# Softmax over window offsets on all 128 partitions of stage 3, with spreads on four row tiles and without GpSimd

## The reference

```python
qkv = x @ w_qkv
starts = jnp.arange(0, L - KS + 1, ST)          # KS = 4, ST = 2
idx = starts[:, None] + jnp.arange(KS)[None, :]
win = qkv[:, idx]
...
dots = jnp.einsum('bnqhd,bnkhd->bnhqk', q, k) * scale
attn = jax.nn.softmax(dots, axis=-1)
o = jnp.einsum('bnhqk,bnkhd->bnqhd', attn, v)
y = o @ w_out + b_out
out = out.at[:, idx.reshape(-1), :].add(y.reshape(B, N * KS, C))
```

## Time and profile before

| | |
|---|---|
| median of 3 executions | 803.98 us (803.6 to 805.56) |
| the profiled execution | 795.91 us, span 794.1 us |
| PE busy | 718.8 us (91%) |
| DVE busy | 492.0 us (62%) |
| ACT busy | 398.2 us (50%) |
| POOL busy | 109.0 us (14%) |
| mean granted TensorE clock | 0.975 |

### The profile page before, as it was taken

How to read it: one execution, slowest core, us unless ns; L and a number is a source line. 1 busy time by engine, 2 the same in 40 slices (tenths; PEclk the granted TensorE clock), 3 DMA queues, 4 the chain that set the end, 5 groups by cost and what they waited for, 6 DMA issues and landing times.

```text
span 794.1 us, 18851 instructions
## 1 busy us (share of the span) xinstructions
PE 718.8 (91%) x7725; PEld 372.5 (47%) x7725; DVE 492.0 (62%) x1136; ACT 398.2 (50%) x732; POOL 109.0 (14%) x103
## 2 busy tenths in 40 slices
PE   6899999986999878999968869999998899999996
PEld 3454545453555543444426445555655334443332
DVE  0673544445889867667557876666664666728552
ACT  2737474735676753434442324656554435553454
POOL 1380313120000000000023544112110000000000
PEclk9999999998999999999977999999999999999998
DMA  8400000000000013552200000000000000000000
GB/s 352 168 4 1 3 0 3 1 4 1 2 2 0 1 30 80 108 109 61 47 0 1 1 0 1 2 4 4 3 4 3 0 1 0 0 1 0 14 14 26
DMA packets 6863, 21.00 MB, mean 26 GB/s; under 512 B 576, under 2 KB 576, under 8 KB 6272
## 3 DMA queue, kind: packets, MB, share of 16 engines
q1 hardware_dynamic: 6784, 19.88, 8.7%
HBM read 18.70 MB, written 1.18 MB: 25 GB/s over the span
## 4 chain that ended last, share of the span: by engine, by line
PE 66%; DVE 16%; ACT 7%; issue 7%; DMA 2%; POOL 1%; DVEq 0%; SPq 0%; ACTq 0%
PE bank L1771 5%; PE bank L2370 4%; PE bank L2296 4%; PE bank L2009 4%; PE bank L1802 3%; PE bank L2349 3%; PE bank L2306 3%; PE bank L1997 3%; PE bank L2002 3%; PE bank L2131 2%; PE bank L1815 2%; DVE sb_rowmax L1135 2%; PE bank L2192 2%; PE bank L2196 2%; PE bank L2285 2%
## 5 line engine op out<-in xcount | busy, mean ns | idle before, releaser
L1771 PE MATMUL bank<-sb_xT,sb_arena 128*128 128x512 f32 x128 | 58.9, 608 | 6.5 <-DMA sb_arena<-w 6.5
L887 ACT ACTIVATE sb_arena<-bank 128x512 f32<-128x512 f32 x64 | 34.8, 607 | 48.5 <-PE bank L2162 48.5
L1451 DVE TENSOR_REDUCE sb_rowmax<-bank 128x4 f32<-128x512 f32 x64 | 41.2, 685 | 23.6 <-PE bank L2153 23.6
L616 ACT ACTIVATE sb_arena<-bank 128x512 f32<-128x512 f32 x64 | 36.1, 601 | 28.3 <-PE bank L1771 28.1
L1065 DVE TENSOR_TENSOR sb_arena<-bank,sb_arena 128x512 f32<-128x512 f32 x32 | 20.9, 686 | 46.0 <-PE bank L1815 46.0
L791 ACT ACTIVATE sb_arena<-bank 128x512 f32<-128x512 f32 x36 | 21.5, 597 | 47.4 <-PE bank L1997 47.4
L531 POOL TENSOR_TENSOR sb_arena<-sb_la,sb_consts 128x1024 f32<-128x1024 f32 x16 | 31.6, 1982 | 88.7 <-PE bank L1802 69.3
L1771 PEld LDWEIGHTS bank<-sb_xT,sb_arena 128*128 128x128 f32 x128 | 24.7, 195 | 37.4 <-issue 35.7
L1684 DVE TENSOR_TENSOR sb_arena<-sb_arena,bank 128x512 f32<-128x512 f32 x32 | 21.0, 683 | 29.7 <-PE bank L2353 22.0
L2009 PE MATMUL bank<-sb_arena,sb_w 128*128 128x512 f32 x72 | 36.0, 600 | 3.0 <-DVE sb_arena L1352 3.0
L742 ACT ACTIVATE sb_arena<-sb_arena 128x512 f32<-128x512 f32 x32 | 20.1, 629 | 35.6 <-DVE sb_arena L1140 35.5
(11 more groups left out here) (338 smaller groups left out, 1602.5 us busy)
## 6 DMA issues: line engine op xcount, KB each, us to landing
sb_arena<-weights_by_expert SPq DMA_DIRECT2D x16, 512.0 KB, 8.0
sb_w<-w SPq DMA_DIRECT2D x1, 2646.5 KB, 22.4
sb_w<-w SPq DMA_DIRECT2D x1, 1736.0 KB, 16.3
sb_consts<-consts SPq DMA_DIRECT2D x1, 1404.0 KB, 10.6
sb_arena<-w SPq DMA_DIRECT2D x2, 512.0 KB, 5.5
sb_ctxT<-ctx SPq DMA_DIRECT2D x1, 1024.0 KB, 12.5
out<-sb_xT SPq DMA_DIRECT2D x4, 256.0 KB, 2.5
sb_xT<-x SPq DMA_DIRECT2D x1, 768.0 KB, 7.9
```

What stands on the lines that cost most here:

```text
L616: act.activation(BC[:, n, :], bank[(4, 5, 0, 1)[n % 4]][:], ACT.Copy).then_inc(s_vev, 1)
L887: act.activation(probT4[k % 2][:, g].rearrange("p b j q -> p (b j q)"), by_key[g][:], ACT.Exp).then_inc(s_e4, 1)
L1451: dve.tensor_reduce(rowmax4[k % 2][:, 4 * g:4 * g + 4], bank[n][:].rearrange("p (j t) -> p j t", j=4), AX, ALU.max).then_inc(s_mx4, 1)
L1771: pe.matmul(bank[(4, 5, 0, 1)[n % 4]][:], bc_w_tiles[:, n, :], cols(c), start=True, stop=True).then_inc(s_v, 1)
```

## The change

In stage 3 only, but for the loop:

- A chunk is cut into 16 blocks of 32 tokens. The head sums put block 4j + s (j column tile, s = 0 to 3) on partitions 32j + 8s to 32j + 8s + 7, so that all 128 partitions hold useful numbers, and an offset takes 32 columns of one bank. The sums of one offset are 16 matmuls of 32 columns, four of which (s) add into the same 32 partitions, each with a stationary matrix that is zero but for its 8 of 32 columns: 96 matmuls in place of 24.
- DVE reads the sums from the bank itself; ACT's copy is gone. All softmax operations work on a quarter of the elements per partition. The exponent is one instruction.
- POOL's three operations on the weights move to DVE, and POOL's pair additions are gone; in their place PE projects six products instead of three. POOL has nothing left in a round.
- The spreads read 32 partitions each (row tile j, weights of 32x128) and write bank j: 16 matmuls of 128 columns for offsets 4, 5, 0, 1, and 16 of 64 columns for 2 and 3. The weighted products then read four banks in strips of 32 columns.
- v is kept in 16 blocks of 36 columns; ACT copies it in two operations.
- The output projection stands in the chunk's own front, the identity matmul and two projections ahead of the next chunk's head sums, four behind. The variance matmul of the chunk before stands behind the second spread.
- The loops of stages 1 and 3 are written out.
- The banks are one tensor with views; the constants change with the layout.

```diff
-            if front in (fronts[0], fronts[2]):
-                for c in range(1, NCH - 1):
-                    front(c, lambda part: tail(c - 1, part), lambda piece: pre(c + 1, piece))
-            else:
-                with eng.Fori(1, NCH - 1) as c:
-                    front(c, lambda part: tail(c - 1, part), lambda piece: pre(c + 1, piece))
+            for c in range(1, NCH - 1):
...
+    win = take(8 * BLOCK).rearrange("p (w o t) -> p w o t", w=2, o=4)
+    win_flat = win.rearrange("p w o t -> p (w o t)")
+    wmax, wden, winv3 = (take(2 * BLOCK).rearrange("p (w t) -> p w t", w=2) for _ in range(3))
     wv = take(6 * CHUNK).rearrange("p (o n) -> p o n", o=6)
-    wvs = take(3 * CHUNK).rearrange("p (o n) -> p o n", o=3)
-    head_spread = const("head_spread").rearrange("p (k n) -> p k n", k=4)
+    head_sum = const("head_sum").rearrange("p (s n) -> p s n", s=4)
+    head_spread = const("head_spread").rearrange("p (s n) -> p s n", s=4)
+    sums3 = bank[4][:, 0:6 * BLOCK].rearrange("p (o t) -> p o t", o=6)
+    spread3 = banks[:, 0:4 * CHUNK].rearrange("p (s n) -> p s n", s=BLOCKS)
+
+    OFFSETS = (4, 5, 0, 1, 2, 3)
...
-        def pre3(c, piece):
-            if piece == 4:
-                wait(pool, s_wi, c + 1)
-                pool.tensor_tensor(winv3, winv3, in_ab, ALU.mult).then_inc(s_wb, 1)
-                wait(pool, s_wb, c + 1)
-                pool.tensor_tensor(win, win, winv3.unsqueeze(2).to_broadcast([P, 2, 4, P]), ALU.mult).then_inc(s_wn, 1)
-                wait(pool, s_wn, c + 1)
-                pool.tensor_tensor(win[:, 0, 0:2, :], win[:, 0, 0:2, :], win[:, 1, 2:4, :], ALU.add).then_inc(s_wa, 1)
...
-            for n in range(3):
-                wait(pool, s_wv, 6 * c + 2 * n + 2)
-                wait(pool, s_po3, c)
-                pool.tensor_tensor(wvs[:, n], wv[:, 2 * n], wv[:, 2 * n + 1], ALU.add).then_inc(s_wvs, 1)
-            nxt(4)
...
-            if piece == 2:
-                for n, (a, b) in enumerate(((0, 4), (4, 6))):
-                    wait(act, s_hs3, 2 * c + n + 1)
-                    wait(act, s_wx, 2 * c)
-                    act.activation(sco[:, a:b, :].rearrange("p o n -> p (o n)"), bank[2 + n][:, 0:(b - a) * P], ACT.Copy)\
-                       .then_inc(s_hs_read, 1)
+                v = bank[5][:].rearrange("p (b t) -> p b t", b=SEQS)
+                halves = lv.rearrange("p (b i) t -> p b i t", i=2)
+                act.activation(halves[:, :, 0, 2:BLOCK + 4], v[:, :, 0:BLOCK + 2], ACT.Copy)
+                act.activation(halves[:, :, 1, 0:BLOCK + 2], v[:, :, BLOCK - 2:], ACT.Copy).then_inc(s_c3, 1)
             if piece == 3:
-                for n in range(2):
-                    wait(act, s_wx, 2 * c + n + 1)
-                    act.activation(win[:, n], win[:, n], ACT.Exp).then_inc(s_we, 1)
+                wait(act, s_wx, 2 * c + 2)
+                act.activation(win_flat, win_flat, ACT.Exp).then_inc(s_we, 1)
...
-                for piece in range(1, 5):
+                for piece in (1, 3, 4):
                     pre3(0, piece)
+            else:
+                hook(1)
             nxt(0)
             if not is_first(c):
-                hook(1)
-            nxt(2)
+                hook(2)
             nxt(1)
             nxt(3)
-            if not is_first(c):
-                hook(2)
             nxt(4)
...
-                wait(dve, s_hs_read, 2 * c + 2)
+                wait(dve, s_hs3, c + 1)
                 for n, a in enumerate((2, 0)):
-                    dve.tensor_reduce(wmax[:, n], sco[:, a:a + 4, :].rearrange("p o n -> p n o"), AX, ALU.max).then_inc(s_wm, 1)
+                    dve.tensor_reduce(wmax[:, n], sums3[:, a:a + 4, :].rearrange("p o t -> p t o"), AX, ALU.max).then_inc(s_wm, 1)
             if piece == 2:
-                wait(dve, s_sp, 6 * c)
+                wait(dve, s_sp, 2 * c)
...
-                    dve.tensor_tensor(win[:, n], sco[:, a:a + 4, :], wmax[:, n].unsqueeze(1).to_broadcast([P, 4, P]),
+                    dve.tensor_tensor(win[:, n], sums3[:, a:a + 4, :], wmax[:, n].unsqueeze(1).to_broadcast([P, 4, BLOCK]),
                                       ALU.subtract).then_inc(s_wx, 1)
             if piece == 3:
+                wait(dve, s_we, c + 1)
                 for n in range(2):
-                    wait(dve, s_we, 2 * c + n + 1)
-                    dve.tensor_reduce(wden[:, n], win[:, n].rearrange("p o n -> p n o"), AX, ALU.add).then_inc(s_ws, 1)
+                    dve.tensor_reduce(wden[:, n], win[:, n].rearrange("p o t -> p t o"), AX, ALU.add).then_inc(s_ws, 1)
+            if piece == 4:
+                wait(dve, s_wi, c + 1)
+                dve.tensor_tensor(winv3, winv3, in_ab, ALU.mult).then_inc(s_wb, 1)
+                wait(dve, s_wb, c + 1)
+                dve.tensor_tensor(win, win, winv3.unsqueeze(2).to_broadcast([P, 2, 4, BLOCK]), ALU.mult).then_inc(s_wn, 1)
+                wait(dve, s_wn, c + 1)
+                dve.tensor_tensor(win[:, 0, 0:2, :], win[:, 0, 0:2, :], win[:, 1, 2:4, :], ALU.add).then_inc(s_wa, 1)
 
...
+
+            def weighted(n):
+                wait(dve, s_sp, 2 * c + 1 + n // 4)
+                if n == 0:
+                    wait(dve, s_c3, 3 * c + 3)
+                    wait(dve, s_po3, c)
+                o, at = OFFSETS[n], BLOCK * (n % 4)
+                v = lv[:, :, o:o + BLOCK - 1:2].unsqueeze(3).to_broadcast([P, BLOCKS, BLOCK // 2, 2])
+                dve.tensor_tensor(wv[:, n].rearrange("p (s m i) -> p s m i", s=BLOCKS, i=2),
+                                  spread3[:, :, at:at + BLOCK].rearrange("p s (m i) -> p s m i", i=2), v, ALU.mult)\
+                   .then_inc(s_wv, 1)
+
+            hook(0)
             if is_first(c):
-                hook(0)
                 pre3(0, 0)
                 hook(1)
-                for piece in range(1, 4):
+                for piece in range(1, 5):
                     pre3(0, piece)
+            for n in range(4):
+                weighted(n)
             nxt(0)
-            if not is_first(c):
-                hook(0)
-            for n in range(6):
-                if n == 0:
-                    wait(dve, s_c3, 3 * c + 3)
-                    wait(dve, s_wvs, 3 * c)
-                wait(dve, s_sp, 6 * c + n + 1)
-                o = (0, 1, 4, 5, 2, 3)[n]
-                v = lv[:, :, o:o + 63:2].unsqueeze(3).to_broadcast([P, SEQS, SEQ // 2, 2])
-                dve.tensor_tensor(wv[:, n].rearrange("p (b m i) -> p b m i", b=SEQS, i=2),
-                                  bank[(5, 0, 1)[n % 3]][:].rearrange("p (b m i) -> p b m i", b=SEQS, i=2), v, ALU.mult)\
-                   .then_inc(s_wv, 1)
-                if n == 2:
-                    nxt(1)
-                if n == 3:
-                    nxt(2)
-            nxt(3)
+            for n in range(4, 6):
+                weighted(n)
             if not is_first(c):
                 hook(1)
+            for piece in range(1, 5):
+                nxt(piece)
...
+            def project(n, to):
+                pe.matmul(bank[to][:], w(3, "wqkv")[:, n * P:(n + 1) * P], cols(c), start=True, stop=True).then_inc(s_q3, 1)
+
             if piece == 0:
-                wait(pe, s_hs_read, 2 * c)
                 wait(pe, s_x, 2 * NCH + c + 1)
-                for n in range(3):
-                    if n == 2:
-                        wait(pe, s_c3, 3 * c)
-                    pe.matmul(bank[2 + n][:], w(3, "wqkv")[:, n * P:(n + 1) * P], cols(c), start=True, stop=True).then_inc(s_q3, 1)
+                wait(pe, s_wx, 2 * c)
+                project(0, 4)
+                wait(pe, s_c3, 3 * c - 1)
+                project(1, 6)
+            if piece == 2:
+                wait(pe, s_c3, 3 * c)
+                project(2, 5)
             if piece == 1:
+                wait(pe, s_c3, 3 * c + 2)
                 for o in range(6):
                     wait(pe, s_qk, 6 * c + o + 1)
-                    if o == 0:
-                        wait(pe, s_c3, 3 * c + 2)
-                    for k in range(TILES):
-                        mm = pe.matmul(bank[2 + o // 4][32 * k:32 * k + 32, (o % 4) * P:(o % 4 + 1) * P], const("head_sum"),
-                                       qk[:, o, k * P:(k + 1) * P], start=True, stop=True)
-                    if o in (3, 5):
-                        mm.then_inc(s_hs3, 1)
+                    for s in range(4):
+                        for j in range(4):
+                            at = BLOCK * (4 * j + s)
+                            mm = pe.matmul(bank[4][32 * j:32 * j + 32, BLOCK * o:BLOCK * o + BLOCK], head_sum[:, s, :],
+                                           qk[:, o, at:at + BLOCK], start=(s == 0), stop=(s == 3))
+                mm.then_inc(s_hs3, 1)
 
         def front3(c, hook, nxt):
+            def spread(part):
+                a, n = ((2, 4), (0, 2))[part]
+                if part == 0:
+                    wait(pe, s_wn, c + 1)
+                    wait(pe, s_wv, 6 * c)
+                else:
```

(60 more changed lines are left out.)

43 lines of the change are left out of this document (20 added, 23 removed).

## The result

| | before | after |
|---|---|---|
| median, first comparison | 803.79 us (4 runs) | 791.64 us (789.39 to 793.17, 4 runs) |
| median, run again | 803.27 us (11 runs) | 793.09 us (791.06 to 797.18, 6 runs) |
| span of the profiled execution | 794.1 us | 791.4 us |
| stage 3, first q, k, v product to stage 4's fillers | 92.07 us | 84.35 us |

The ratio is 0.9848 (95% interval 0.9811 to 0.9885) in the first comparison and 0.9871 (0.9837 to 0.9904) in the second: faster by 12.2 and 10.2 us, where 21 were forecast. 791.64 lies in the range of 776 to 795, and 8.6 us above the 783 of the forecast.

The account below looks back on a forecast made before the run. A chain, no full engine, was taken to bound stage 3. After the change PE's order sums to 15.0 us a round against 18.8; stage 4's fillers start at 467.6 against 488.56, 21 us less: 783 us, range 776 to 795.

Parts of the forecast that it names:

- chain of softmax operations: Stage 3, from first maximum to first spread of a chunk: 3.7 us on DVE with 128 partitions, against 9.4 before.
- the six products: Stage 3's q-times-k products on DVE: 3.7 us without POOL's product beside them, against 6.30 and 6.01 before.
- the spreads on four row tiles: Stage 3, 16 matmuls of 128 and 16 of 64 columns: 0.86 us taken for each of the two parts.
- rival 2: Stage 3's row tiles don't overlap in f32: 3.7 us instead of 0.86 for each of eight spreads; 805 us; chance 0.07.
- the wait for the logarithm: Each stage 3 round: the identity matmul writes the variance's bank and waits for the logarithm, 0.8 us of PE idleness.
- PE's order: Stage 3: the sequence of PE work and waits bounds a round at 15.0 us, against 18.8; DVE needs 12.7.
- the head sums: Stage 3, 96 matmuls of 32 columns at 28 ns each: 2.7 us a chunk, bounds 1.35 and 5.4, before 1.56.
- Rival 1: Small matmuls cost double: records at 28 ns, stage 3's head sums 5.4 us; 791 us in all; chance 0.13.
- written-out code at no cost: Loops of stages 1 and 3 written out: stage 1 put at nothing; 0.35 us of issue in stage 3 expected to go, uncounted.
- the end at full clock: Stage 3, last chunk's first spread to stage 4's fillers: 14.3 us, including 2.5 us of DVE with nothing to project.
- rival 3: TensorE's clock stays at half through stage 3, small tiles and waits leaving the array too idle: 831 us; chance 0.05.

Follow-up runs that it names:

- with 16 matmuls: The changed kernel with the head sums of all six offsets in 16 matmuls of 192 columns instead of 96 of 32; 782.5 us, ratio to before 0.9737.
- with fillers: On the changed kernel with 16 head-sum matmuls of 192 columns: 30 unread matmuls (7, 13, 10) put into three idle stretches of TensorE; 776.13 us, ratio to before 0.9668.

## Why the prediction came out as it did

**The mechanism was right, and the size was not.** Stage 3 was bound by a chain, and the change cuts it. The chain of softmax operations is 3.36 us (forecast 3.7, before 9.41); the six products are 3.70; the spreads on four row tiles overlap (32 records in 1.17 and 1.12 us, forecast 0.86), so rival 2 is out; the wait for the logarithm is 0.78 (forecast 0.8). The first maximum waits for PE, not for ACT. PE's order is the bound, at 14.99 us in the fourth stretch (forecast 15.0). That sum is right by two errors: the head sums cost 1.76 us from start to next start and not 2.7, while the two spreads take 2.15 and not 1.72, the variance matmul 1.13 and not 0.86, and q, k, v with the three matmuls ahead of the sums 5.54 and not 5.16. The spreads' 0.86 us had been taken against the prediction's own lower bound of 0.93 us for 16 matmuls of 128 columns. The norm and the copies on DVE and ACT lie beside, as said. The two rounds of stage 1 took 50.22 us in the changed kernel and 50.17 before, from one chunk's copies (L1086, before L1109) to those two chunks on.

**The head sums were mis-sized, on the good side.** 28 ns for each of 96 matmuls became 1.83/96 = 19 ns, or 9.5 ns a record. Rival 1 (records at 28 ns, 5.4 us) is out, although its 791 us is the time that was measured: the agreement is chance. By the overhead of about 60 cycles a matmul that the Trainium skill, TensorEngine Tiling (Array Packing), section Performance Considerations, gives, they would take 2.4 us at least, an estimate. The trace is below that, so the measurement decides, and in this case the rule doesn't hold for four column tiles taken together.

**The step that failed: written-out code at no cost.** The prediction put the written-out loops at nothing and said that slower fetching would show as issue time in stage 1, and its round of 15.0 us had no term for the supply of instructions. In stage 1 PE has one idle time of 0.41 us so marked, and the rounds kept their length. The supply shows in the stage that at the same time got four times as many head-sum matmuls. A set of 192 records and their loads is 384 instructions in 1.8 us, more than one packet of 256, while PE goes on 2.4 to 2.6 us behind the start of the packet on the queue. Neither half does it alone: the stalls of chunks 1 and 2 go with 16 matmuls, with the loops, and with the written-out code moved by 122 instructions. 2.67 and 2.49 us are lost in the second and third stretch, 1.65 in the first; 12.06 less 1.65 is 10.4, and 10.6 was forecast. Behind the stall in the second stretch the clock fell again (0.68 from 427.15 to 432.48 us): the eight records there took 5.40 us in place of 3.70, in both profiles. Behind the third stretch's stall it stayed up, for a reason that these runs don't show. 16.2 (forecast) + 2.7 + 1.7 - 0.9 (cheaper sums) = 19.7, and 19.83 were measured.

**The second step that failed: the end at full clock.** The prediction saw that there is nothing to project between the last two spreads, and charged 2.5 us of DVE time, but not what an idle PE does to the clock. Granted clock is 0.74 in the last stretch. PE idles 2.70 us, then spread, variance, and the three matmuls take 1.92, 2.85 with the wait, and 5.04 us against 0.86, 1.66 and 2.58: 4.7 of the 5.4 us. Some 4.0 of them are the clock, since with fillers the same end took 15.80 us at full clock; the rest is what these steps cost above the forecast at full clock too. In the earlier trace rows this end had PE busy 12.50 of 12.50 us; the change made the idle. This is rival 3 in small: the clock fell in three places (412.65, 427.15 and 469 us), the first of which the forecast had in it, and in the rounds of chunks 1 and 2, with PE busy 14 of 15 and of 18 us, it stayed at 1.00. The Trainium skill, TensorE: Matmul & The Clock Gate, Part 1, says that the low clock is the default and that activity lifts it; the fillers agree, which do no useful work and left the clock at 1.00 in every stretch of the stage.

**The sum.** 1.5 + 3.6 + 2.7 + 5.4 = 13.2 us more in stage 3 than forecast, 84.35 and not 71.1. The median missed by 8.6 only, and that it lies in the range is in part luck: the range reached so far for rival 1, whose mechanism is out, and outside the stage a gain came that was not forecast. The stage's gain in the profiles was 7.7 and 9.4 us, the medians' 12.2 and 10.2. The difference lies outside the stage, which took 702.0 and 711.0 us in the two profiles of before, 707.0 and 706.7 in those of after. Why these stretches differ from execution to execution, and whether the change has a part of some 2 us in it, stays open. So does, for chunks 0 and 1 of the kernel with loops, whether the place of the code alone keeps the stalls away.

## What to carry to other kernels

Cost short matmuls by instructions too: where more than one packet of code (here 256 instructions, a load and a matmul for each record) is consumed in less time than a packet takes to come (two stalls 256 instructions apart, in chunk 0 with 125 matmuls added, ended 3.46 us apart), PE stands still with the releaser "issue", and one matmul with a strided operand in place of six removes it. The mark is no proof by itself. The test is to put instructions ahead: a stall that keeps its place in the instruction list, and so meets another matmul, is the instruction supply. When a chain gets shorter, look for the places where PE now has nothing to do: filling three of them, here at the start and at the end of the stage, was worth 6.4 us in the medians, half of what the change gave. And read a stage's time from more than one profile where the clock falls within it: the same end took 15.80 us once and 18.67 to 20.27 otherwise.

## What the hardware showed that was not expected

- PE's instructions arrive in packets of 16 KB, 256 instructions. The stalls in stage 3 sit 256 or a multiple of it apart, end 2.2 to 2.7 us after the packet's start on the queue, and are 0.6 to 2.7 us long. The second pass of a loop started no packet from 445.5 to 458.5 us.
- Adding 61 useless matmuls made a kernel 4.6 us faster (stage 3 took 77.10 us in place of 84.35 and 82.74); with 125 the stalls were back, at the same places of the list.
- f32 matmul records of 32 columns on four column tiles take 9.5 ns each (192 in 1.83 us), whole-array ones of 512 columns 0.46 us (8 in 3.70 us).
- 2.70 us without PE work (466.4 to 469.1 us) was followed by a granted clock of 0.55, 0.50 and 0.67 in the three stretches of 4 us from 468 to 480 us. The same idle was followed by full clock in one profile of six.
- GpSimd's product of 128x1024 took 2.34 us and stretched VectorE's six products from 3.7 to 6.0 us; on VectorE it took 1.23.
